# A row of maxima moved from one PSUM pair to the other, two more residual tiles, and a new order of five engines

## The reference

```
x = x + attn(layernorm(x))
x = x + xattn(layernorm(x), ctx)
x = x + ffn(layernorm(x))

xattn: scores = einsum('bhqd,bhkd->bhqk', q, k) * scale
       scores = where(causal, scores, -inf)
       out = einsum('bhqk,bhkd->bhqd', softmax(scores), v); return out @ Wo.T
ffn:   w = the two best of sigmoid(x @ Wr), divided by their sum
       hid = silu(x @ Wg) * (x @ Wu), weighted by w; routed = hid @ Wd + skips
       return routed + causal_conv4(x)
```

## Time and profile before

| | |
|---|---|
| median of 3 runs | 196.93 us (196.34 to 197.08) |
| the profiled execution | 196.06 us, of which the span is 194.3 us |
| busy: TensorE, VectorE, ScalarE, GpSimd | 166.0, 163.4, 124.9, 113.8 us |
| granted clock, mean | 0.991 |
| largest groups | VectorE reductions of maxima 58.5 us (48), ScalarE exponentials 49.0 us (48), GpSimd masks 37.5 us (48) |

### The profile page before, as it was taken

The page is one execution under the profiler, slowest core; times in us unless marked ns, Lnnn a source line. Parts: engine busy times, 40 slices in busy tenths (PEclk is TensorE's granted clock), DMA queues, the critical chain, the costliest instruction groups (busy, mean ns, idle before and its releaser), DMA issues.

```text
span 194.3 us, 5501 instructions
## 1 busy us (share of the span) xinstructions
PE 166.0 (85%) x1812; PEld 114.5 (59%) x1812; DVE 163.4 (84%) x458; ACT 124.9 (64%) x281; POOL 113.8 (59%) x204
## 2 busy tenths in 40 slices
PE   6958697778898899995999999988988998797973
PEld 6846484545566556672866576656646546554542
DVE  6665878847787889998999989999999799399893
ACT  2036563528857798785776398858976568756560
POOL 7864877951932873798236633657366167754432
PEclk9999999969999999999999999999999999999999
DMA  5931131120332210013203211232121000000001
GB/s 174 321 142 41 36 84 48 46 69 15 97 83 57 59 32 21 1 46 107 71 4 83 60 48 31 55 86 57 44 59 33 27 7 2 27 3 0 30 2 54
DMA packets 17796, 11.00 MB, mean 57 GB/s; under 512 B 2388, under 2 KB 17108, under 8 KB 17768
## 3 DMA queue, kind: packets, MB, share of 16 engines
q1 hardware_dynamic: 17768, 10.66, 18.7%
HBM read 3.10 MB, written 1.05 MB: 21 GB/s over the span
## 4 chain that ended last, share of the span: by engine, by line
DVE 29%; PE 23%; issue 21%; POOL 18%; ACT 6%; DVEq 1%; POOLq 0%; ACTq 0%
DVE negmax L839 7%; PE max_pair L966 4%; POOL rstd L488 4%; POOL xn L498 4%; PE ffn_bank L966 4%; PE self_bank L966 4%; PE pv_bank L966 4%; DVE convT L944 3%; ACT probs L641 3%; POOL probs L524 2%; DVE stats L735 2%; PE soft_pair L966 2%; POOL hid L533 2%; POOL vareps L480 1%; POOL xres L506 1%
## 5 line engine op out<-in xcount | busy, mean ns | idle before, releaser
L839 DVE TENSOR_REDUCE negmax<-max_pair 128x4 f32<-128x1024 f32 (+1 forms) x48 | 58.5, 1218 | 6.6 <-PE max_pair L966 6.1
L641 ACT ACTIVATE probs<-soft_pair 128x1024 f32<-128x1024 f32 x48 | 49.0, 1020 | 8.8 <-PE soft_pair L966 8.8
L524 POOL TENSOR_SCALAR_AFFINE_SELECT probs<-probs 128x512 f32<-128x512 f32 (+1 forms) x48 | 37.5, 795 | 21.8 <-ACT probs L641 21.8
L966 PE MATMUL pv_bank<-probs,vs 128*32 128x128 f32 (+1 forms) x512 | 23.7, 328 | 1.6 <-POOL probs L524 1.4
L966 PEld LDWEIGHTS pv_bank<-probs,vs 128*32 128x32 f32 x512 | 14.4, 109 | 10.6 <-POOL probs L524 3.7
L966 PE MATMUL soft_pair<-qs,ks 64*128 64x256 bf16 (+1 forms) x256 | 18.9, 247 | 1.1 <-ACT probs L641 1.0
L966 PE MATMUL max_pair<-causal,picks 64*128 64x128 bf16 (+1 forms) x192 | 15.5, 240 | 4.8 <-DVE negmax L839 3.2
L606 ACT ACTIVATE xn<-x,shift,rstd 128x128 f32<-128x128 f32 x32 | 14.0, 488 | 8.4 <-DVE shift L759 8.4
L966 PE MATMUL max_pair<-ks,qs 64*128 64x128 bf16 (+1 forms) x256 | 18.8, 245 | 0.0
L488 POOL TENSOR_TENSOR rstd<-vareps,exponent 128x2 f32<-128x2 f32 x24 | 17.4, 725 | 2.0
L533 POOL TENSOR_TENSOR hid<-hraw,cw 128x256 f32<-128x256 f32 x16 | 10.3, 649 | 13.6 <-DVE hraw L921 7.1
(11 more groups left out here) (195 smaller groups left out, 386.8 us busy)
## 6 DMA issues: line engine op xcount, KB each, us to landing
ks<-kparts SPq DMA_DIRECT2D x48, 64.0 KB, 2.0
qs<-qparts SPq DMA_DIRECT2D x48, 64.0 KB, 2.1
out_dram<-result SPq DMA_DIRECT2D x8, 128.0 KB, 1.8
loaded<-packed_dram SPq DMA_DIRECT2D x1, 768.0 KB, 7.7
loaded<-packed_dram SPq DMA_DIRECT2D x1, 640.0 KB, 8.8
qs<-maxparts SPq DMA_DIRECT2D x32, 4.0 KB
loaded<-packed_dram SPq DMA_DIRECT2D x1, 462.5 KB, 6.3
loaded<-packed_dram SPq DMA_DIRECT2D x2, 192.0 KB, 3.0
```

The costliest lines, as they stand in the source:

```text
L524: nc.gpsimd.affine_select(out=v, in_=v, compare_op=ALU.is_ge, fill=0.0, base=0, pattern=[[0, n], [1, P]], channel_multiplier=-1).then_inc( ...
L641: nc.scalar.activation(probs[b.par][g][:, k, :], soft_pair[:, :], ACT.Exp).then_inc(exp_done, 1)
L839: nc.vector.tensor_reduce(maxima, max_pair[:, :].rearrange("p (u h k) -> p u h k", u=2, h=n), AX.X, ALU.max, negate=True).then_inc(max_rea ...
L966: return nc.tensor.matmul(out, lhsT, rhs, start=start, stop=stop, skip_group_check=True)
```

## The change

Four edits and a new ORDER for all five engines.

1. The row of maxima is transposed into soft_pair instead of max_pair, so max_pair is used by units of maxima and their reductions alone. max_mid now counts on a semaphore of its own, maxmid_done. The row stands between two soft units: it waits for the exponential two units before the first unit that needs it (ROW_LEAD), and the soft unit behind it waits for max_mid.
2. Four tiles x2 instead of two, with the waits of residual2 moved from two batches back to four.
3. In the last batch soft units 3 and 5 write into max_pair, which has been read for the last time by then, and each unit from the fifth on waits for the exponential two before it instead of the one before. The gate and up products of that batch, which use max_pair too, wait for the last exponential.
4. The convolution matmuls are a step of their own, ffn_conv, ahead of ffn_down; in batches 6 and 7 they need not wait for ScalarE's copy of hid.

The code part of the diff, cut to the lines that differ and the functions they are in:

```diff
-        x2 = two("x2_", [P, T, C])
+        x2 = [sb(f"x2_{i}", [P, T, C]) for i in range(4)]
...
-        vs_done, pe_soft, exp_done, masked, pe_max, max_read, pe_maxrow, maxhi_done = sems(
-            "vs_done pe_soft exp_done masked pe_max max_read pe_maxrow maxhi_done")
+        vs_done, pe_soft, exp_done, masked, pe_max, max_read, pe_maxrow, maxhi_done, maxmid_done = sems(
+            "vs_done pe_soft exp_done masked pe_max max_read pe_maxrow maxhi_done maxmid_done")
...
-        PER_BATCH = UNITS + 2
+        ROW_LEAD = 2
...
+        def pair_of_soft(b, u):
+            return max_pair if b.c == B - 1 and u in (3, 5) else soft_pair
...
             def send_max(b, g):
-                sp.wait_ge(max_read, b.count(PER_BATCH, 4 * (g + 1)))
+                sp.wait_ge(maxmid_done, b.count(2, g + 1))
...
-                    source = {2: x1[b.c % 4], 3: x2[b.par]}[n]
+                            act.wait_ge(relu7_done, b.count(2, -2))
+                    source = {2: x1[b.c % 4], 3: x2[b.c % 4]}[n]
...
-                nc.scalar.activation(probs[b.par][g][:, k, :], soft_pair[:, :], ACT.Exp).then_inc(exp_done, 1)
+                nc.scalar.activation(probs[b.par][g][:, k, :], pair_of_soft(b, u)[:, :], ACT.Exp).then_inc(exp_done, 1)
             def max_high(b, g):
-                nc.scalar.copy(maxparts[g][:, 0, :], max_pair[0:16, 0:P]).then_inc(maxhi_done, 1)
+                nc.scalar.copy(maxparts[g][:, 0, :], soft_pair[0:16, 0:P]).then_inc(maxhi_done, 1)
...
             def source(n, b):
-                return {1: x_of(b), 2: x1[b.c % 4], 3: x2[b.par]}[n]
+                return {1: x_of(b), 2: x1[b.c % 4], 3: x2[b.c % 4]}[n]
...
-                nc.vector.tensor_tensor(maxparts[g][:, 1, :], max_pair[0:16, 0:P],
-                                        maxparts[g][:, 0, :], ALU.subtract).then_inc(max_read, 1)
+                nc.vector.tensor_tensor(maxparts[g][:, 1, :], soft_pair[0:16, 0:P],
+                                        maxparts[g][:, 0, :], ALU.subtract).then_inc(maxmid_done, 1)
...
             def residual2(b, _):
-                if b.since(2):
-                    dve.wait_ge(xn_done[3], b.count(2, -2))
-                    dve.wait_ge(skip_done, b.count(2, -2))
-                nc.vector.tensor_tensor(x2[b.par][:, :, :], pv_bank[:, 0:S].rearrange("p (t c) -> p t c", t=T),
+                if b.since(4):
+                    dve.wait_ge(xn_done[3], b.count(2, -6))
+                    dve.wait_ge(skip_done, b.count(2, -6))
+                nc.vector.tensor_tensor(x2[b.c % 4][:, :, :], pv_bank[:, 0:S].rearrange("p (t c) -> p t c", t=T),
...
-                                                       in1=x2[b.par][:, t, :], op0=ALU.mult, op1=ALU.add).then_inc(skip_done, 1)
+                                                       in1=x2[b.c % 4][:, t, :], op0=ALU.mult, op1=ALU.add).then_inc(skip_done, 1)
...
-                n = PER_BATCH * b.c + u + g
+                n = UNITS * b.c + u
...
             def maxrow(b, g):
-                pe.wait_ge(max_read, b.count(PER_BATCH, 4 * g + 3))
-                nc.tensor.transpose(max_pair[0:16, 0:P], negmax[:, g, :, :, :].rearrange("p u h t -> p (u h t)"),
+                pe.wait_ge(max_read, b.count(UNITS, 3 * g + 3))
+                if b.c or g:
+                    pe.wait_ge(exp_done, b.count(UNITS, 3 * g - ROW_LEAD))
+                nc.tensor.transpose(soft_pair[0:16, 0:P], negmax[:, g, :, :, :].rearrange("p u h t -> p (u h t)"),
...
-                if n:
+                row, left = divmod(n + ROW_LEAD, 3)
+                if n == 0:
+                    pe.wait_ge(maxmid_done, 1)
+                elif left == 0 and row < 2 * B:
+                    pe.wait_ge(maxmid_done, row + 1)
+                if b.c == B - 1 and u == 3:
+                    pe.wait_ge(max_read, UNITS * B)
+                elif b.c == B - 1 and u > 3:
+                    pe.wait_ge(exp_done, n - 1)
+                elif n:
...
-                        bank = soft_pair[:, 512 * half:512 * half + 512].rearrange("p (h q) -> p h q", h=heads)
+                        bank = pair_of_soft(b, u)[:, 512 * half:512 * half + 512].rearrange("p (h q) -> p h q", h=heads)
...
             def ffn_gate_up(b, t):
-                    pe.wait_ge(max_read, PER_BATCH * B)
+                    pe.wait_ge(exp_done, UNITS * B)
...
+            def ffn_conv(b, _):
+                pe.wait_ge(conv_done, b.count(KC - 1, KC - 1))
+                pe.wait_ge(hidT_done if b.c < B - 2 else hid0_done, b.count(1, 1) if b.c < B - 2 else b.count(2, 2))
+                for t in range(T):
+                    mm(bank_of_ffn(b, "down")[:, t * C:(t + 1) * C], convT[b.par][:, t * P:(t + 1) * P], ident[:, :], start=t == 0, stop=False)
             def ffn_down(b, _):
-                pe.wait_ge(conv_done, b.count(KC - 1, KC - 1))
-                    o = bank_of_ffn(b, "down")[:, t * C:(t + 1) * C]
-                    mm(o, convT[b.par][:, t * P:(t + 1) * P], ident[:, :], stop=False)
-                        ins = mm(o, hidT[b.par][:, i, t * P:(t + 1) * P], w["down"][:, i * C:(i + 1) * C], start=False, stop=i == 1)
+                        ins = mm(bank_of_ffn(b, "down")[:, t * C:(t + 1) * C], hidT[b.par][:, i, t * P:(t + 1) * P],
+                                 w["down"][:, i * C:(i + 1) * C], start=False, stop=i == 1)
-                     maxrow, pv, out_t, o2_t, o_proj, ffn_x_t, ffn_router, ffn_gate_up, ffn_hid_t, ffn_down)
+                     maxrow, pv, out_t, o2_t, o_proj, ffn_x_t, ffn_router, ffn_gate_up, ffn_hid_t, ffn_conv, ffn_down)

```

More of the change, by code:

```diff
@@ new lines @@
+        self_out.2.0 cross_k_v.1.0 self_proj.1.0 self_sum.3.0 self_o_t.2.0 self_out.3.0 self_proj.2.0 max.0.0
+        cross_norm_t.1.0 self_o_t.3.0 max.0.1 cross_q2.1.0 self_proj.3.0 max.0.2 cross_k_v.2.0 maxrow.0.0
+        max.0.3 self_x_t.4.0 self_q1.4.0 max.0.4 soft.0.0 max.0.5 self_kv.4.0 cross_norm_t.2.0 maxrow.0.1
+        max.1.0 soft.0.1 cross_q2.2.0 max.1.1 soft.0.2 self_sum.4.0 max.1.2 soft.0.3 cross_k_v.3.0 maxrow.1.0
+        max.1.3 soft.0.4 self_out.4.0 max.1.4 soft.0.5 pv.0.0 soft.1.0 max.1.5 pv.0.1 max.2.0 self_o_t.4.0
@@ new lines @@
+        out_t.0.0 maxrow.1.1 self_proj.4.0 max.2.1 o2_t.0.0 soft.1.1 o_proj.0.0 cross_norm_t.3.0 soft.1.2
+        max.2.2 self_x_t.5.0 cross_q2.3.0 soft.1.3 self_q1.5.0 max.2.3 maxrow.2.0 cross_k_v.4.0 ffn_x_t.0.0
+        max.2.4 soft.1.4 pv.1.0 soft.1.5 max.2.5 ffn_router.0.0 self_kv.5.0 ffn_gate_up.0.0 soft.2.0 max.3.0
+        pv.1.1 maxrow.2.1 self_sum.5.0 max.3.1 soft.2.1 out_t.1.0 self_out.5.0 cross_norm_t.4.0 soft.2.2 max.3.2
+        o2_t.1.0 cross_q2.4.0 self_o_t.5.0 soft.2.3 o_proj.1.0 self_proj.5.0 cross_k_v.5.0 maxrow.3.0
@@ new lines @@
+        self_x_t.6.0 max.3.3 soft.2.4 self_q1.6.0 ffn_gate_up.0.1 soft.2.5 max.3.4 self_kv.6.0 pv.2.0 soft.3.0
+        max.3.5 pv.2.1 max.4.0 maxrow.3.1 self_sum.6.0 ffn_hid_t.0.0 out_t.2.0 max.4.1 soft.3.1 self_out.6.0
+        cross_norm_t.5.0 o2_t.2.0 ffn_conv.0.0 ffn_down.0.0 cross_q2.5.0 max.4.2 soft.3.2 self_o_t.6.0
+        o_proj.2.0 ffn_x_t.1.0 self_proj.6.0 max.4.3 soft.3.3 ffn_router.1.0 self_x_t.7.0 cross_k_v.6.0
+        maxrow.4.0 max.4.4 self_q1.7.0 ffn_gate_up.1.0 soft.3.4 max.4.5 self_kv.7.0 soft.3.5 ffn_gate_up.1.1
@@ new lines @@
+        max.5.0 soft.4.0 pv.3.0 pv.3.1 maxrow.4.1 self_sum.7.0 ffn_hid_t.1.0 out_t.3.0 soft.4.1 max.5.1
+        self_out.7.0 ffn_conv.1.0 ffn_down.1.0 o2_t.3.0 cross_norm_t.6.0 max.5.2 soft.4.2 o_proj.3.0
+        cross_q2.6.0 ffn_x_t.2.0 soft.4.3 max.5.3 ffn_router.2.0 self_o_t.7.0 maxrow.5.0 ffn_gate_up.2.0
+        self_proj.7.0 soft.4.4 max.5.4 cross_k_v.7.0 soft.4.5 ffn_gate_up.2.1 max.5.5 soft.5.0 pv.4.0 maxrow.5.1
+        pv.4.1 ffn_hid_t.2.0 soft.5.1 max.6.0 ffn_conv.2.0 ffn_down.2.0 soft.5.2 max.6.1 ffn_x_t.3.0 out_t.4.0
@@ new lines @@
+        cross_norm_t.7.0 ffn_router.3.0 max.6.2 soft.5.3 ffn_gate_up.3.0 o2_t.4.0 cross_q2.7.0 maxrow.6.0
+        o_proj.4.0 max.6.3 soft.5.4 ffn_gate_up.3.1 soft.5.5 max.6.4 pv.5.0 soft.6.0 max.6.5 pv.5.1 maxrow.6.1
+        max.7.0 soft.6.1 ffn_hid_t.3.0 out_t.5.0 max.7.1 soft.6.2 ffn_conv.3.0 ffn_down.3.0 o2_t.5.0 soft.6.3
+        max.7.2 ffn_x_t.4.0 o_proj.5.0 ffn_router.4.0 max.7.3 maxrow.7.0 ffn_gate_up.4.0 soft.6.4 max.7.4
+        soft.6.5 ffn_gate_up.4.1 max.7.5 soft.7.0 pv.6.0 maxrow.7.1 pv.6.1 soft.7.1 ffn_hid_t.4.0 out_t.6.0
```

200 lines of the change are left out of this document (88 added, 112 removed).

## The result

The changed kernel takes 187.48 us (median of 4 runs, 187.33 to 188.5); the kernel before took 196.63 beside it (4 runs, 194.9 to 197.08). The ratio is 0.9561, 95% interval 0.9493 to 0.9629. Run again later, it took 187.27 (6 runs, 187.14 to 188.18) against 196.62, ratio 0.9534 (0.9490 to 0.9578). The profiled execution took 187.55 us, span 185.8; before it was 196.06, span 194.3, so 8.5 us of span are to be explained.

A forecast was written before the change was run, and what follows sets the result against it. VectorE (94% busy) and TensorE (92%) were taken to fill the middle, leaving gains where VectorE's list stalls. Terms -1.2 - 3.0 + 0.2 - 1.0 = -5.0 us gave 191.06 profiled, 191.9 as median; range 187.0 to 198.0.

The forecast's parts named there:

- The start: Up to the first reduction: batch 0's self_out ahead of batch 2's transposition, less one clear; -1.2 us, ends 0 and -2.1.
- The stage to batch 1's third reduction: From 31.39 to 51.22 us: batch 4's normalisation on time, row out of the max chain; -3.0, ends -1.2 and -5.4.
- By rows that wait is short: Early stage: soft unit 0.0's wait for its row's transfer brings no slow clock; otherwise -1.5 instead of -3.0 us.
- The middle: 51.22 to 160.54 us: 2.3 us of row waits go, soft units wait instead; +0.2, ends -2.3 and +2.6.
- From the last reduction: From 160.54 us: o_proj earlier, batch 6's work done earlier, convolution beside the copy; -1.0, ends +1.0 and -3.2.
- two waits of 0.47 that cancel against 0.9: Batch 7: units 7.3 and 7.5 skip an exponential wait of 0.47 each, offsetting unit 7.1's +0.9 us.
- Batch 6's work that VectorE has done earlier: After the last reduction: VectorE has done some of batch 6's work already, worth -0.5 us.
- The convolution, priced at -0.5: Last down projection: its two convolution matmuls run beside ScalarE's copy, -0.5 us.
- The row that holds up soft units: Rival, middle: late subtraction delays soft units, exponentials, masks and pv; +7.5 instead of +0.2, 199.2 us; chance 0.15.
- VectorE stretched by GpSimd: Rival, middle: more overlaps with GpSimd lengthen VectorE instructions by 4.3 us, 196.2, no change; chance 0.11.
- An early lead waited away: Rival: being 4 us early at 51.22 only makes later waits; 1.0 stays, 195.9 us, no change; chance 0.09.
- More goes than I count: Rival, 51.22 to 160.54 us: half of VectorE's idle time goes too, another 4.2 us, 187.7; chance 0.13.

The follow-up runs named there:

- roots_late: Changed kernel with GpSimd's old order around 28 to 39 us, so batch 4's normalised tile comes after the low parts: 193.53 us, ratio 0.9860.
- order_only: Changed kernel with row back in max_pair, units of maxima behind rows, last batch's soft units in soft_pair, convolution waiting for the copy everywhere: ratio 1.0479.
- row_only: Kernel before with only the row of maxima moved to soft_pair, and five soft units put behind a row on TensorE: 207.76 us, ratio 1.0518.
- after_again: The changed kernel, unaltered, run again later: 187.27 us, ratio 0.9534.
- tail_back: Changed kernel with the last batch's soft units all in soft_pair and the convolution waiting for ScalarE's copy of hid in every batch: 190.08 us, ratio 0.9693.
- two_tiles: Changed kernel with two x2 tiles instead of four, and batch 5's skip ahead of batch 7's residual on VectorE: 188.24 us, ratio 0.9602.
- soft_back: Changed kernel with only the last batch's soft units put back, all in soft_pair: 189.36 us, ratio 0.9644.
- conv_back: Changed kernel with the convolution of batches 6 and 7 again waiting for ScalarE's copy of hid: 187.87 us, ratio 0.9553.
- no_run_ahead: Changed kernel, row still in soft_pair, with eight units of maxima put behind the row and seven reductions behind max_mid: 194.16 us, ratio 0.9893.
- four_moves: Changed kernel with four order moves: self_kv.4 ahead of soft.0.0, max.1.0 ahead of a row, two convolution taps earlier at the end: 189.17 us, ratio 0.9610.

## Where the prediction was right and where it was wrong

The 187.48 us lie in the range, 0.5 above its lower end, and 4.4 below the forecast. By stretches the middle gave 4.5 us more than was forecast and the end 1.2 less; the other two came out as forecast.

**The start, -1.2 forecast, -1.37 measured: right in kind, so close by luck.** VectorE's denominators come at 14.20 where they came at 15.92, and nothing is idle before them:

```profile
14.20 0.13 DVE L806 TENSOR_SCALAR den<-self_bank 128x32 f32<-128x32 f32 x1
```

But the first transposition came earlier, too, and its start varies by over a microsecond between profiles of one list (above). Before, then after:

```profile
8.08 0.38 PE L970 MATMUL self_bank<-ident,xn 128*128 128x128 f32 x2
```

```profile
7.24 0.38 PE L976 MATMUL self_bank<-ident,xn 128*128 128x128 f32 x2
```

The first reduction varies with it only in part. Under the new list it starts at 30.02 to 30.91 in ten profiles (all but those of roots_late and order_only, both 31.08); under the old one at 31.39 in before and at 31.19 in row_only, whose list is the old one up to there. So the order gives between 0.1 and 1.4 us, inside the ends that were given, and a single pair of profiles can't tell it more closely.

**The stage to batch 1's third reduction, -3.0 forecast, -2.99 measured: the cause was right, so close by luck.** Batch 4's normalised tile is on time, and when it was made late (roots_late), the stage lost 5.25 us and the end 6.3 by the medians. In seven profiles with the changed kernel's list up to there the stage takes 15.71 to 17.00 us, which is 2.8 to 4.1 less than before. The half clock remained, though, from 39 to 42 us in place of 41 to 44, behind a wait of 1.08 us of soft unit 0.0 for its row's transfer:

```profile
38.83 0.54 PE L972 MATMUL soft_pair<-qs,ks 64*128 64x256 bf16 x4 [1.08 <-DMA qs<-maxparts]
```

"By rows that wait is short" was therefore too sure. What the half clock costs can't be told. The stage takes 16.77 to 16.84 us in the three profiles that have it there (after, after_again, tail_back), and 15.71, 16.35, 16.76 and 17.00 in the four that do not (two_tiles, soft_back, conv_back, no_run_ahead). Of the ten executions of the changed kernel the two with a mean clock of 0.991 took 187.26 and 187.55 us, the others 187.14 to 188.5. The Trainium skill, "TensorE: Matmul & The Clock Gate", section "The HAM clock gate", has the slow clock as the default, which activity lifts; the trace agrees in that the slow stretch follows a wait of TensorE, but the stage gave -2.99 with it, not the -1.5 worked out by that rule.

**The middle, +0.2 forecast, -4.31 measured: the step that failed.** It read: "the nearest row is the old wait, 3.0 us for 16 rows, which would just have changed engines". The old wait did not change engines; it was covered. Soft units waited 0.6 us in the middle, and max_mid 0.8 where it waited 2.1. I had taken the two chains apart and found neither full, and from this that nothing was to be had; what I did not count is that eight rows now have the next unit of maxima ahead of them on TensorE, and seven of these its reduction ahead of max_mid on VectorE, work of 1.2 us that fills the time in which the row travels. no_run_ahead prices that at 6.9 us, more than the whole gain, but under the new lists. Against the kernel before, the covered wait is 1.3 of the 4.31 us and VectorE's busy time 2.85, of which 0.92 is moved work and 1.3 shift; which move shortened the rest was not run. Running ahead would not have been possible with the row in max_pair as that kernel waited, since a unit then has to wait for max_mid, which stands behind the unit's own reduction. The busy time that VectorE lost by less stretching (1.3 us on shift alone) was not in my sum either; I had held it a rival in the other direction.

**From the last reduction, -1.0 forecast, +0.17 measured.** The 2.90 us that batch 6's residual waited for o_proj are gone, as forecast, but 1.28 come back at the instruction ahead of it, which waits for batch 4's down product; the stretch is 0.97 shorter. VectorE in order of time, after:

```profile
159.50 0.42 DVE L958 TENSOR_TENSOR result<-ffn_bank,base 128x256 f32<-128x256 f32 x1 [1.28 <-PE ffn_bank L972]
159.95 0.42 DVE L876 TENSOR_TENSOR x<-pv_bank,x 128x256 f32<-128x256 f32 x1
```

Three more mistakes lie behind it. The soft units were priced at two waits of 0.47 that cancel against 0.9; they save two of 1.12, and soft_back makes it 2.1 us. "Batch 6's work that VectorE has done earlier" is the reverse: VectorE's list has behind the last reduction all that it had there, and four steps for batch 4 more. On TensorE pv.6.0 stands behind the last unit of maxima now, and pv.6.1 behind the row. That holds soft unit 7.1 up: it starts 2.91 us after the last reduction (151.87), where it started 1.49 us after it (160.54), which is 1.4 later and not 0.9. TensorE in order of time, before and then after:

```profile
160.34 1.51 PE L966 MATMUL pv_bank<-probs,vs 128*32 128x256 f32 x32
...
162.03 0.39 PE L966 MATMUL soft_pair<-qs,ks 64*128 64x256 bf16 x4
```

```profile
153.34 1.51 PE L972 MATMUL pv_bank<-probs,vs 128*32 128x256 f32 x32
154.78 0.39 PE L972 MATMUL soft_pair<-qs,ks 64*128 64x256 bf16 x4
```

The second pair makes up for most of it: batch 7's last exponential starts 9.97 us after the last reduction, before 9.48. That a list with pv.6.1 ahead of the row would keep the 2.1 us was not run. The convolution, priced at -0.5, is worth 0.3 in the two profiles and cannot be told in the medians. It does run beside ScalarE's copy, but in the last batch it now waits for VectorE's last tap instead (0.63 us, before 0.68 for the copy):

```profile
181.45 0.71 PE L972 MATMUL max_pair<-ident,convT 128*128 128x128 f32 x4 [0.63 <-DVE convT L950]
```

**The rivals.** The row that holds up soft units was a real danger: it is what row_only (5.8 us in 8 waits) and four_moves (1.30 in one) ran into; the new order keeps clear of it. VectorE stretched by GpSimd went the other way. An early lead waited away: roots_late excludes it, since a delay there is not taken up later. "More goes than I count" came to 187.7, next to the result, but by its mechanism it should have halved the 8.5 us that VectorE idles in the middle; they fell by 1.46. Two of the signs of being right failed: VectorE's waits for the row came to 2.3 us in the whole run, not below 1.5, and the half clock lasted as long as before.
